# Causal attention inside a layer kernel on one core: scores and maxima from two fp32r parts in two 64-row tiles, instead of three bf16 parts in 96 rows

## The reference, cut to what matters

```python
def _L0_attn_ref(x, W_Q, W_K, W_V, W_o):      # T = 4096 tokens, D = 256, 16 heads of 16
    Q, K, V = (heads(W_Q), heads(W_K), heads(W_V))
    scores = jnp.einsum('bhqd,bhkd->bhqk', Q, K) / D_HEAD ** 0.5
    causal = jnp.triu(jnp.full((S, S), -jnp.inf, dtype=scores.dtype), k=1)
    scores = scores + causal
    probs = jax.nn.softmax(scores, axis=-1)
    out = jnp.einsum('bhqk,bhkd->bhqd', probs, V)
    return out.transpose(0, 2, 1, 3).reshape(B, S, D_MODEL) @ W_o

xn = _layernorm(x, axis=-1)
x = x + _L0_attn_ref(xn, ...) + _L0_ffn_ref(xn, ...)   # the second: 16 experts, each picks its top 512 tokens
```

## Time and profile before

| what | us |
|---|---|
| median of 3 runs | 2676.88 |
| the three runs | 2676.87 to 2677.44 |
| profiled execution: span from first to last instruction | 2677.5 |
| of it: project, up to the first matmul of attend | 134 |
| FIRST, the maxima of the first three stretches | 58 |
| the four groups of heads | 1676 |
| all that follows | 809 |
| busy in the whole span: PE, DVE, ACT, POOL | 2522.1, 2001.2, 1450.4, 270.1 |

### The profile page before, as it was taken

How to read it: one execution, slowest core, us unless ns; L and a number is a source line. 1 busy time by engine, 2 the same in 40 slices (tenths; PEclk the granted TensorE clock), 3 DMA queues, 4 the chain that set the end, 5 groups by cost and what they waited for, 6 DMA issues and landing times. The chain is left out here.

```text
span 2677.5 us, 47674 instructions
## 1 busy us (share of the span) xinstructions
PE 2522.1 (94%) x15166; PEld 1274.3 (48%) x15166; DVE 2001.2 (75%) x3915; ACT 1450.4 (54%) x1931; POOL 270.1 (10%) x215
## 2 busy tenths in 40 slices
PE   7689999999999999999999999998899599999997
PEld 4323333333333333333333333332788488888886
DVE  6588999877899967899978899981655366666664
ACT  4406666665666675666676666668222345455453
POOL 2420000000000000000000000000110133333322
PEclk9859999999999999999999999999999799999999
DMA  7740000021000012000012100000221444444444
GB/s 232 241 119 23 11 9 9 9 60 46 9 15 4 8 49 58 17 9 9 9 29 58 34 5 3 3 3 6 77 70 39 167 124 116 115 115 115 123 123 125
DMA packets 159113, 160.68 MB, mean 60 GB/s; under 512 B 40896, under 2 KB 142784, under 8 KB 158912
## 3 DMA queue, kind: packets, MB, share of 16 engines
q1 hardware_dynamic: 146240, 139.76, 16.6%
q0 software_dynamic: 12672, 18.42, 4.1%
HBM read 115.50 MB, written 42.24 MB: 59 GB/s over the span
## 5 line engine op out<-in xcount | busy, mean ns | idle before, releaser
L792 DVE TENSOR_REDUCE a_mp<-a_pm 128x1 f32<-128x512 f32 (+3 forms) x2304 | 1334.2, 638 | 178.4 <-PE a_pm L873 96.1
L851 ACT ACTIVATE a_p<-a_ps 128x1024 f32<-128x1024 f32 (+3 forms) x1152 | 1039.1, 950 | 669.7 <-PE a_ps L911 438.7
L873 PE MATMUL a_pm<-a_k,a_q 96*128 96x512 bf16 (+3 forms) x2304 | 756.3, 375 | 47.9 <-DVE a_mp L792 25.0
L911 PE MATMUL a_ps<-a_q,a_k 99*128 99x512 bf16 (+3 forms) x2304 | 658.2, 364 | 14.0 <-issue 6.9
L924 PE MATMUL a_po<-a_p,a_v 128*32 128x512 f32 (+3 forms) x4608 | 574.2, 571 | 0.1
L873 PEld LDWEIGHTS a_pm<-a_k,a_q 96*128 96x128 bf16 x2304 | 202.3, 97 | 745.2 <-DVE a_mp L792 617.3
L911 PEld LDWEIGHTS a_ps<-a_q,a_k 99*128 99x128 bf16 x2304 | 213.2, 99 | 209.5 <-ACT a_p L851 77.1
L1315 DVE TENSOR_TENSOR e_hf<-e_g,e_pu 128x512 f32<-128x512 f32 x128 | 88.0, 688 | 174.7 <-ACT e_g L1272 174.7
L1348 PE MATMUL e_pg<-e_xt,e_wgup 128*128 128x512 f32 x768 | 198.9, 394 | 12.6 <-DVE e_xt L1298 12.6
L1272 ACT ACTIVATE e_g<-e_pg 128x512 f32<-128x512 f32 x128 | 76.6, 599 | 245.1 <-PE e_pu L1348 245.1
L1358 PE MATMUL e_po<-e_wdp,e_hp 128*128 128x256 f32 x1536 | 203.3, 284 | 0.0
(11 more groups left out here) (154 smaller groups left out, 1725.4 us busy)
## 6 DMA issues: line engine op xcount, KB each, us to landing
e_wgu<-in_wg SPq DMA_DIRECT2D x18, 1024.0 KB, 5.6
e_wgu<-in_wu SPq DMA_DIRECT2D x18, 1024.0 KB, 7.8
e_wd<-in_wd SPq DMA_DIRECT2D x18, 1024.0 KB, 10.2
qk_parts<-p_parts SPq DMA_DIRECT2D x32, 384.0 KB, 2.8
a_q<-qk_parts SPq DMA_DIRECT2D x192, 64.0 KB, 2.3
a_k<-qk_parts SPq DMA_DIRECT2D x192, 64.0 KB, 2.3
v_padded<-p_v SPq DMA_DIRECT2D x8, 1024.0 KB, 5.5
a_v<-v_padded SPq DMA_DIRECT2D x32, 256.0 KB, 3.0
```

The source lines that it names most:

```text
L792: eng.tensor_reduce(MP[j % 2][:, h * NB + r, kc:kc + 1], ps[:, 0:w], AX.X, ALU.max).then_inc(s_mf, 1)
L851: eng.activation(PR[b % 2][:, 2 * a:2 * a + 2, off:GT], pS[a][:, :].rearrange("p (h n) -> p h n", h=2)[:, :, off:GT], ACT.Exp).then_inc(s_ ...
L873: last = eng.matmul(ps[:, 0:w], q, KT[0:KR, h, kc * GT:kc * GT + w], start=True, stop=kc < j)
L911: last = eng.matmul(pS[a][:, col + off:col + GT], KT[0:KM, h, b * P:(b + 1) * P], QT[SLOT[j]][0:KM, h, off:GT], start=True, stop=b < NB * j)
```

## The change: what it does

- Q and K are split into two parts of type fp32r (4 bytes) instead of three of bf16: ACT writes the first, DVE the second straight away. The buffer `R`, ACT's second pass and GpSimd's pass go. A store carries 2 x 4 bytes for each value instead of 3 x 2.
- A score is the sum of three products (high x high, high x low, low x high): 48 rows; with the maximum in two parts 50 (`KM`). Heads are taken in pairs: one in partitions 0 to 49, the other in 64 to 113 of the same buffers. The two matmuls of a pair address different 64-row tiles of the array and different banks.
- The list of units has the two heads of a pair next to each other (the index i).
- The causal mask is added within a row tile: its 128 contraction rows are given in two halves (`half[m]`, `maskqk[m]`, `maskkq[m]`), so that there are two mask matmuls of 64 rows where there was one of 128.
- The maximum is split in two parts by two DVE instructions instead of four, and stored by four transfers (two parts, two tiles) instead of three. `plan` prices it 700 instead of 1200.
- The rows of ones for the maximum are written before K arrives, in 16 pieces that span the third product's rows too, and SP waits for the pieces of a stretch before it fetches its K.

```diff
-TERMS = [(0, 0), (0, 1), (1, 0), (1, 1), (0, 2), (2, 0)]
+TERMS = [(0, 0), (0, 1), (1, 0)]
 KR = len(TERMS) * DH
-KM = KR + 3
+KM = KR + 2
+HALF = P // 2
...
-        PTS = [c.sb(f"p_parts{s}", [P, 4, 3, GT], BF16) for s in range(2)]
-        R = c.sb("p_rest", [P, 4, GT])
+        PTS = [c.sb(f"p_parts{s}", [P, 4, 2, GT], F32R) for s in range(2)]
...
-                        eng.wait_ge(s_lo, 4 * g + m + 1)
-                        eng.scalar_tensor_tensor(out=R[:, m, :], in0=pQ[m][:, :], scalar=0.25 if m < 2 else 1.0,
-                                                 in1=PTS[s][:, m, 0, :], op0=ALU.mult,
-                                                 op1=ALU.subtract).then_inc(s_r, 1)
+                        eng.scalar_tensor_tensor(out=PTS[s][:, m, 1, :], in0=pQ[m][:, :],
+                                                 scalar=0.25 if m < 2 else 1.0,
+                                                 in1=PTS[s][:, m, 0, :].bitcast(F32), op0=ALU.mult,
+                                                 op1=ALU.subtract).then_inc(s_lo, 1)
...
-                    for m in range(4):
-                        eng.wait_ge(s_r, 4 * g + m + 1 + 4)
-                        eng.copy(PTS[s][:, m, 1, :], R[:, m, :]).then_inc(s_mid, 1)
...
-                        eng.tensor_tensor(PTS[s][:, m, 2, :], R[:, m, :], PTS[s][:, m, 1, :],
-                                          ALU.subtract).then_inc(s_lo, 1)
...
-            return [(h, r, kc) for kc in range(j + 1) for h in range(HG) for r in range(NB)]
+            return [(a, r, kc, i) for kc in range(j + 1) for a in range(2) for r in range(NB) for i in range(2)]
...
-            return {"max": 1200, "out": 1000, "bit": 2000}[u[0]]
+            return {"max": 700, "out": 1000, "bit": 2000}[u[0]]
...
+                    eng.wait_ge(s_one, 2 * n + 2)
                     fetch_kv(eng, 0, n)
...
-                eng.memset(KT[KR:KM, :, :], 1.0).then_inc(s_one, 1)
-                eng.wait_ge(s_one, 1)
+                for n in range(NQ):
+                    for i in range(2):
+                        eng.memset(KT[i * HALF + 2 * DH:i * HALF + KM, :, n * GT:(n + 1) * GT].bitcast(F32),
+                                   1.0).then_inc(s_one, 1)
+                        eng.wait_ge(s_one, 2 * n + i + 1)
...
                         eng.tensor_copy(nb[:, 0, :], ps[0:HG * NB, 0:P]).then_inc(s_sp, 1)
-                        eng.wait_ge(s_sp, 2 * turned(g, j) + 1)
-                        eng.tensor_tensor(R1[:, :], ps[0:HG * NB, 0:P], nb[:, 0, :], ALU.subtract).then_inc(s_mf, 1)
-                        eng.wait_ge(s_mf, (g * PER + F if g is not None else 0) + n + 1 + 3)
-                        eng.tensor_copy(nb[:, 1, :], R1[:, :]).then_inc(s_sp, 1)
-                        eng.wait_ge(s_sp, 2 * turned(g, j) + 2)
-                        eng.tensor_tensor(nb[:, 2, :], R1[:, :], nb[:, 1, :], ALU.subtract).then_inc(s_nb, 1)
+                        eng.wait_ge(s_sp, turned(g, j) + 1)
+                        eng.tensor_tensor(nb[:, 1, :], ps[0:HG * NB, 0:P], nb[:, 0, :].bitcast(F32),
+                                          ALU.subtract).then_inc(s_mf, 1)
...
-                        q = QT[SLOT[j]][0:KR, h, r * P:(r + 1) * P]
-                        last = eng.matmul(ps[:, 0:w], q, KT[0:KR, h, kc * GT:kc * GT + w], start=True, stop=kc < j)
+                        tile, lo = slice(i * HALF, i * HALF + KR), slice(i * HALF, (i + 1) * HALF)
+                        q = QT[SLOT[j]][tile, a, r * P:(r + 1) * P]
+                        last = eng.matmul(ps[:, 0:w], q, KT[tile, a, kc * GT:kc * GT + w], start=True, stop=kc < j)
                         if kc == j:
-                            last = eng.matmul(ps[:, w - P:w], k.identb[:, :], k.maskqk[:, :], start=False, stop=True)
+                            for m in range(2):
+                                last = eng.matmul(ps[:, w - P:w], k.half[m][lo, :], k.maskqk[m][lo, :],
+                                                  start=False, stop=m == 1)
...
-                        for h in (2 * a, 2 * a + 1):
-                            col = (h % 2) * GT
-                            last = eng.matmul(pS[a][:, col + off:col + GT], KT[0:KM, h, b * P:(b + 1) * P],
-                                              QT[SLOT[j]][0:KM, h, off:GT], start=True, stop=b < NB * j)
-                            if b >= NB * j:
-                                last = eng.matmul(pS[a][:, col + off:col + off + P], k.identb[:, :],
-                                                  k.maskkq[:, :], start=False, stop=True)
+                        for i in range(2):
+                            tile, col = slice(i * HALF, i * HALF + KM), i * GT
+                            last = eng.matmul(pS[a][:, col + off:col + GT], KT[tile, a, b * P:(b + 1) * P],
+                                              QT[SLOT[j]][tile, a, off:GT], start=True, stop=b < NB * j)
+                        if b >= NB * j:
+                            for m in range(2):
+                                for i in range(2):
+                                    lo, col = slice(i * HALF, (i + 1) * HALF), i * GT
+                                    last = eng.matmul(pS[a][:, col + off:col + off + P], k.half[m][lo, :],
+                                                      k.maskkq[m][lo, :], start=False, stop=m == 1)
...
-        k.qkd = nc.dram_tensor("qk_parts", (2, 3, D, T), BF16, kind="Internal").ap()
+        k.qkd = nc.dram_tensor("qk_parts", (2, 2, D, T), F32, kind="Internal").ap()
```

More of the change, by code:

```diff
@@ L94, in constants @@
     k.identf = k.sb("identf", [P, P])
-    k.identb = k.sb("identb", [P, P], BF16)
+    k.half = [k.sb(f"half{n}", [P, P], BF16) for n in range(2)]
     k.before = k.sb("before", [P, P], BF16)
@@ L98, in constants @@
     k.onesb = k.sb("onesb", [P, P], BF16)
-    k.maskqk = k.sb("maskqk", [P, P], BF16)
-    k.maskkq = k.sb("maskkq", [P, P], BF16)
+    k.maskqk = [k.sb(f"maskqk{n}", [P, P], BF16) for n in range(2)]
+    k.maskkq = [k.sb(f"maskkq{n}", [P, P], BF16) for n in range(2)]
     s = k.sem("s_const")
@@ L104, in _ @@
         def _(eng):
-            fills = [(k.identf, 0.0), (k.identb, 0.0), (k.onesf, 1.0), (k.onesb, 1.0), (k.before, 1.0),
-                     (k.maskqk, 0.0), (k.maskkq, 0.0)]
+            fills = [(k.identf, 0.0), (k.onesf, 1.0), (k.onesb, 1.0), (k.before, 1.0)]
+            fills += [(b, 0.0) for b in (*k.half, *k.maskqk, *k.maskkq)]
             for buf, v in fills:
@@ L119, in _ @@
                                   base=base, channel_multiplier=ch).then_inc(s, 1)
+            for i in range(2):
+                rows = slice(i * HALF, (i + 1) * HALF)
+                eng.wait_ge(s, len(fills) + 2 + 6 * i)
+                for n in range(2):
+                    for buf, op, ch, st, fill in [
+                        (k.half[n], ALU.not_equal, 1, -1, 1.0),
+                        (k.maskqk[n], ALU.is_ge, 1, -1, NEG),
+                        (k.maskkq[n], ALU.is_ge, -1, 1, NEG),
+                    ]:
+                        eng.affine_select(out=buf[rows, :], in_=buf[rows, :], pattern=[[st, P]], compare_op=op,
+                                          fill=fill, base=ch * n * HALF, channel_multiplier=ch).then_inc(s, 1)
 def project(nc, k, x, wq, wk, wv, gate):
@@ L323, in _ @@
                 k.soft.scalar(eng)
-            @block.gpsimd
-            def _(eng):
-                eng.sem_inc(s_lo, 4)
-                def group(i, s):
-                    g = 2 * i + s
-                    for m in range(4):
-                        eng.wait_ge(s_mid, 4 * g + m + 1)
-                        eng.tensor_tensor(PTS[s][:, m, 2, :], R[:, m, :], PTS[s][:, m, 1, :],
-                                          ALU.subtract).then_inc(s_lo, 1)
-                with eng.Fori(0, NG // 2) as i:
-                    for s in range(2):
-                        group(i, s)
             @block.tensor
@@ L599, in attend @@
     with ctx:
-        KT = c.sb("a_k", [KM, HG, T], BF16)
-        QT = [c.sb(f"a_q{n}", [KM, HG, GT], BF16) for n in range(5)]
+        KT = c.sb("a_k", [HALF + KM, 2, T], F32R)
+        QT = [c.sb(f"a_q{n}", [HALF + KM, 2, GT], F32R) for n in range(5)]
         V = c.sb("a_v", [P, NKB, HG * VW])
@@ L605, in attend @@
         NM = [c.sb(f"a_nm{n}", [P, HG * NB]) for n in range(2)]
-        R1 = c.sb("a_r1", [HG * NB, P])
-        NB3 = [c.sb(f"a_nb{n}", [HG * NB, 3, P], BF16) for n in range(5)]
+        NMX = [c.sb(f"a_nb{n}", [HG * NB, 2, P], F32R) for n in range(5)]
         OT = [c.sb(f"a_ot{n}", [P, GT]) for n in range(2)]
@@ L615, in attend @@
         s_q = [c.sem(f"a_sq{n}") for n in range(5)]
-        s_one, s_mb, s_mf, s_nm, s_sp, s_nb = (c.sem(f"a_{n}") for n in ("one", "mb", "mf", "snm", "sp", "snb"))
+        s_one, s_mb, s_mf, s_nm, s_sp = (c.sem(f"a_{n}") for n in ("one", "mb", "mf", "snm", "sp"))
         s_nq = [c.sem(f"a_nq{n}") for n in range(5)]
@@ L714, in store_rows, with store_max @@
```

(10 more changed lines are left out.)

58 lines of the change are left out of this document (28 added, 30 removed).

## The result

| | before | changed |
|---|---|---|
| median, us | 2677.16 | 2768.12 |
| all runs, us | 2676.87 to 2679.13 (4) | 2760.16, 2761.79, 2774.46, 2798.53 |
| ratio | 1 | 1.0359, 95% interval 1.0305 to 1.0413 |
| profiled execution, span | 2677.5 | 2758.4 |
| project, up to the first matmul of attend | 134 | 136 |

The changed kernel is **slower by 91 us**; the forecast was 75 us faster, 2602. The profiled execution is the fastest of the four; its span is 81 us longer than before, of which 78 lie in attend, 2 in project and 1 behind attend. The runs also scatter over 38 us, where the kernel before scatters over 2.

A forecast was written before the change was run, and what follows sets the result against it. DVE was taken to bound the ordinary block, with PE 0.2 us behind. From 2677.5 us, −62 − 18 − 20 + 22 + 3 = −75 gave 2602 us, range 2535 to 2735.

The forecast's parts named there:

- The bound of the ordinary block: Attend's five-unit block: DVE bounds it at 3.17 us; PE's work falls from 2.93 to about 2.5.
- DVE's idle time, −62: Attend: faster PE recovers 52 of 82 us of waits for full units, 10 of 55 for masked ones.
- A pair of scores, 0.26 us: Scores on PE: two row tiles run together, limited by two fp32r loads of 0.128 us each.
- my own sign that I am wrong: Scores on PE: forecast fails if a pair's second matmul starts 0.2 us or more after the first.
- The maximum on DVE, −18: Maxima on DVE: two of four instructions go, saving 0.56 us, 32 times.
- Where ACT is the bound, −20: Groups' bit blocks and the last group's rest without units: 20 us of ACT's 32 us of waits for scores go.
- Masks and short matmuls, +22: Diagonal blocks: doubled masks and short fp32r loads cost 0.8 us for each of 32 diagonals, nearly all on the path.
- FIRST and project, +3: FIRST and project: larger Q and K stores and more masks cost 3 us together, bounds −5 to +15; ones mostly hidden.
- The row tiles take turns: Rival, PE's units and scores: tiles run one after the other, ordinary block 3.2 to 3.3 us, 2752 us total; chance 0.17.
- The clock: Rival: PE stands at 1.2 GHz while waiting for DVE; +50 us with a tenth of blocks, +500 with all; chance 0.05.
- The range: Whole kernel: predicted time lies between 2535 and 2735 us.
- All bounds on one side: Whole kernel: every term at its low or high bound gives 2485 or 2772 us.

The follow-up runs named there:

- e9: The kernel before with the maximum in two bf16 parts instead of three, by two DVE instructions instead of four, priced 700 in the plan: 2671.01 us, ratio 0.9973.
- e6: The changed kernel with bf16 instead of fp32r parts and every row tile filled to 62 and 64 rows: 2590.10 us, ratio 0.967.
- e5: The changed kernel, still fp32r, with every row tile filled to 62 rows for units and 64 for scores by multiplying zeros: 2722.97 us, ratio 1.0176.
- e1: The changed kernel with its two parts of Q, K and the maximum in bf16 instead of fp32r: 2603.69 us, ratio 0.9744.
- e8: e5 with the second scores call of a block moved behind the two units ahead of the product: 2841.30 us, ratio 1.0631.
- e4: The changed kernel with all causal mask matmuls left out, in units and scores: 2714.16 us, ratio 1.0152.
- e2: The kernel before with only three of its six bf16 products (48 rows for a unit, 51 for scores), no row tiles, as many matmuls: 4092.95 us.
- e3: The changed kernel with each pair of score matmuls issued twice, the second overwriting the first: 2782.02 us, ratio 1.0397.
- e7: e5 with one mask matmul over all 128 rows instead of two of 64 within a tile: 2984.62 us, ratio 1.1134.

## Why the prediction was wrong

The medians close as one sum: the maximum in two parts −6.5 (e9), two 64-row tiles with two bf16 parts −80.9 (from e9 to e6), fp32r instead of bf16 +132.9 (to e5), 48 and 50 rows instead of 62 and 64 +45.1 (to the changed kernel). Together +90.6. Another order would share it out somewhat differently: with 48 rows the type costs 164 (e1).

- **The bound of the ordinary block.** DVE was named rightly, with PE close behind. The step that failed is "PE's work falls from 2.93 to about 2.5 us, and DVE's 3.17 stay". I compared sums of work. What decides is the way from a freed bank over the product to the next full bank, 1.84 us against some 1.9 of maxima: it had no slack, and fp32r made it 0.22 longer. The parts of it all stood in the earlier trace rows. e8 shows the way by making it longer, e6 by making it shorter. The load of an open unit even stood in my text, as 0.19 instead of 0.10 us, but as a condition of a rival and not as a term of the sum; it holds whether the tiles take turns or not.
- **DVE's idle time, −62.** 52 behind full units and 10 behind masked ones should have gone. Measured: 96 became 170 and 68 became 102 us. With bf16 (e6) they are 45 and 68: the first is what I had foreseen for full units, so PE does catch up where the loads don't prevent it.
- **A pair of scores, 0.26 us.** It starts 0.25 apart in the block shown (402.19 and 402.45 in the trace), the right number for the wrong reason, and by my own sign that I am wrong (0.2 us or more). The tiles do run together: the two units behind the product, one in each tile, start 0.003 us apart (404.129 and 404.132) and last 0.49 each. But the unit ahead of the pair still streams in one of its tiles, and that member of the pair waits for it. In this order of the queue most scores calls have such a neighbour: of 749 calls of full width with both matmuls in the trace, 591 follow a unit directly, and 234 start together, within 0.01 us.
- **The maximum on DVE, −18.** It is −6.5 (e9), since most of the time saved turned into waits for PE.
- **Where ACT is the bound, −20.** Little of it came. The first 13 blocks of the last stretch, where most bits are, take 31.7 us instead of 32.5 in the second group (from start to start of their exponentials), and from the start of the last unit to the last copy it is 75.8 us instead of 77.9. Four times the one and once the other are 5 us. In all of attend ACT's wait for full scores grew to 513.5 us, where the earlier trace rows has 438.7.
- **Masks and short matmuls, +22.** Too large on the narrowest block, where I counted 0.5 us more: it is 0.63 us from the first scores matmul to the product instead of 0.57 (1038.47, to 1039.04). All masks together are worth 54 us (e4), and with bf16 and doubled masks DVE waits 68.1 us for masked units (e6), as before (67.7). So the doubling isn't seen there; the 102 of the changed kernel came with fp32r and the clock.
- **FIRST and project, +3.** Project took 2 us more. GpSimd's ones were hidden, as said.
- **The rivals.** "The row tiles take turns" gave 2752, nearest to the result, but by a mechanism that isn't there. "The clock", with a chance of 0.05, is right in that it leaves 2.4 GHz within the groups; filling the tiles gave 45 us back, and some 50 us more at 1.2 GHz than before remain in e5. The mechanism wasn't the one that I gave, waiting for DVE: the earlier trace rows has PE busy for 3.00 of 3.00 us at 0.50, and in the new stretches it pauses hardly more (15.86 of 16). I had discounted it because PE hardly pauses; e2 shows that this is no protection.
- **The range.** 2735 left out 33 us. All bounds on one side gave 2772, just above the result: the bounds were sound, the likeliest values weren't.

The rows of the narrowest diagonal block of the changed kernel show the masks at their cheapest: two fp32r scores start 0.17 us ahead of their masks, and from there to the product, with the second call between, it is another 0.46.

```profile
1945.30 0.33 PE L914 MATMUL a_ps<-a_q,a_k 50*128 50x128 f32 x2
1945.47 0.12 PEld L920 LDWEIGHTS a_ps<-maskkq,half 64*128 64x128 bf16 x4
...
1945.93 0.16 PEld L930 LDWEIGHTS a_po<-a_p,a_v 128*32 128x32 f32 x8
```

Still open: why the time of the changed kernel scatters so much more than that of the kernel before. It goes with the stretches at 1.2 GHz (the run of 2798.53 us had a mean clock of 0.922, the profiled one of 0.940), but no run separates the two. Also open is where all of e6's 81 us against e9 come from: DVE's waits for units account for 61 (174.0 to 113.4). fp32r without row tiles wasn't tried. And since the clock fell in e2, what two tiles alone give in bf16 isn't separated from what the clock gives.

## What to carry to other kernels

Two engines that hand a few banks to each other form a loop, and its slack is the time of the maxima in the full banks less the longest way through the other engine's queue. Work that out before summing each engine's work; an operand type whose load takes 0.08 us longer counts there once for every matmul that waits, even where loads in a stream are hidden. And before halving the rows of most matmuls, ask what the granted clock will do: filling the tiles with rows of zeros was worth 45 us with fp32r, 14 with bf16.

## What the runs showed that I had not expected

- The granted clock went with the rows at work, though not with them alone. With 48 of 96 rows and the same matmuls PE stood at 1.2 GHz for nearly all of attend while busy: 4092.95 us against 2677.6 (e2). Rows of zeros help (e5), and so does more streaming (e3) or the same rows in two tiles (e1).
- A matmul that waits for another engine shows its load: 0.49 to 0.50 us with fp32r (load 0.18 to 0.19), 0.39 with bf16 (0.09 to 0.10).
- Two 64-row tiles start 0.003 us apart, but a matmul waits for the one ahead of it in its own tile, and a matmul over the whole array between them finds the loader idle for 0.36 us (e7, the block shown).
